# A two-layer scan kernel: planned times of layer 2's side steps moved by about one slot

## The chip, the cores and the metric

The kernel runs on one core of one Trainium2 chip. The metric is the device time of one launch in microseconds (us), over all 16 images. A core has TensorE (PE in the profile, its weight loads PEld), VectorE (DVE), ScalarE (ACT), GpSimd (POOL) and SyncE (SP), which here only issues DMAs. Each engine works through its own list of instructions in order and waits on semaphores.

## What is computed

The input is x of shape (16, 192, 56, 56). Layer 1 is group norm, an RWKV mixing layer and a residual add; the change does not touch it. Layer 2 is group norm and a Mamba block with a forward and a backward direction, and a residual add. Cut to what matters here:

```
tok = group_norm(x) as 3136 tokens of 192 channels
x1, x2 = layernorm(tok) * g + b                      # two pairs of g, b
x, z = x1 @ W_in_x.T, x2 @ W_in_z.T                  # 384 channels each
branch(x):                                           # once forward, once backward in time
    xc  = silu(conv_b + 4-tap convolution of x)
    dbl = xc @ W_xproj.T                             # 12 rows for dt, 16 for B, 16 for C
    dt  = softplus(dbl[:12] @ W_dt.T + dt_bias)
    h_t = h_(t-1) * exp(dt_t * A) + dt_t * xc_t * B_t  # 384 channels x 16 states
    y_t = sum over the states of h_t * C_t, + xc_t * D
out = x + ((y_forward + y_backward) * silu(z)) @ W_out.T + b_out
```

## The kernel before, in words

A loop over the 16 images holds two blocks, one for each layer; the engines meet between them. Layer 2 cuts the 3136 tokens into 7 chunks of T = 448 and goes over them forward (chunks i = 0 to 6) and then backward (i = 7 to 13): `CHUNK`, NI = 14. The 384 channels are EJ = 3 groups of 128 (e = 0, 1, 2). The 16 states of a group are NP = 8 **slots**, each of two states for 64 channels: an instruction has 128 partitions and 2 x 448 elements. So a chunk has PER = 24 slots, and an image Q = 336, numbered g. "Place n" below is the slot n of its chunk.

**The main line of a slot.** For pair q of slots:
- ScalarE, `decay` (L1294): two exponentials of dt * A, into one of two pairs of PSUM banks, one slot ahead of the scan; then `reset` (L1303) and `carry` (L1311), a few elements each. `decay(q)` waits for scan q-2.
- the product dt * xc * B: on VectorE for odd q (L1148, issued at slot q-2) and on GpSimd for even q (L1355, issued at slot q-3). It goes into one of NB = 4 buffers. VectorE's reads dt * xc from a PSUM bank, which a TensorE step `dp` (L985) fills once per group; GpSimd's reads it from SBUF, where a DMA `ud` (L1440) has spread it.
- VectorE, `scan` (L1159): the recurrence.
- GpSimd, `outputs` (L1364): h * C for two slots at once (q and q+1, q even), issued at slot q+2. It waits for both scans and, as its result has NPR = 4 slots of buffer, for TensorE's sum of the pair before the last (`c_sm >= q - 2`).
- TensorE, the **sum** (L1065), LAG = 2 slots behind: 8 matmul instructions add the two slots of a pair into the y bank, YBANK. A group begins there with the skip product xc * D (L1057), which waits until y of the group before has been read out, and ends, in backward chunks, with y of the forward direction added (L1060).

VectorE's slot is scan, then product (at odd slots), then side steps. ScalarE's is `decay(g+1)`, `reset`, `carry(g-1)`, side steps. GpSimd's is outputs (at even slots), product (at odd slots), side steps. TensorE's is the skip product and the sum (at odd slots), then side steps.

**The side steps** are all else. `side_schedule` gives each a planned time in slots by hand; each engine's list is sorted by it, and `Steps.due(g)` issues, at the end of slot g, what has a planned time below g + 1. So a shift of one slot changes what stands in front of what in an engine's list, and nothing is started by a clock. The steps of chunk i, with t the chunk's start, run while chunk i-1 is scanned:
- forward: `ns`, `n1`, `nc`, `nq`, `n2`, `nr`, `nm` (layer norm, on ScalarE, TensorE L992 and L998, VectorE L1096, ScalarE L1199, GpSimd L1338), `x` and `xe` (the projection L1004 and its copy), `nw`, `xw` (stores)
- both: `cv` (the convolution, 8 matmul instructions, L1018), `c1` to `c4` (ScalarE, L1220 to L1233), `xc` (VectorE, L1122), `xp` (TensorE, L1025), `p1` (ScalarE, L1240), `cw` (stores B and C), `bl` and `cl` (loads that spread them, L1418 and L1424), and for each group `t`, `t1` to `t3`, `td`, `du` (TensorE L1030, ScalarE L1247 to L1255, VectorE L1128, GpSimd L1344), `dd` and `de` (DMAs L1433 that spread dt), `ud` and `dp`
- backward: `z` with `z1` to `z4` and `g` (the gate: TensorE L1035, ScalarE L1266 to L1283, GpSimd L1348), `o` and `ou` (the output projection L1042 and its add, L1140), `xl`, `nl`, `yl`, `out` (loads and the store)
- `ye` reads y of a group out of YBANK: ScalarE (L1259) in forward chunks, VectorE (L1135) in backward ones. In both it waits for the last sum of its group.

Convolutions, projections and gates share two PSUM banks (6 and 7), which a loop at the end of `side_schedule` gives out in the order of the planned times; a step waits until the last reader of its bank is done.

Of the kernel before, what the change touches and what calls it, by code (L numbers as in the profile page):

```python
# [23 lines left out]
PER = EJ * NP  # L24
# [11 lines left out]


AHEAD, LAG = 2, 2
NB, NH, NPR = 4, 6, 4
NXC, NDT, NDU, NR2 = 5, 3, 3, 3  # L40

# [23 lines left out]
def side_schedule():  # L65


    pe, act, dve, pool, sp = [], [], [], [], []

    def conv(i, e, t):  # L70
        if (i, e) == (0, 0):
            dve.append((t, "cd", i, e))
        else:
            pe.append((t, "cv", i, e))
        act.extend([(t + 1.9, "c1", i, e), (t + 2.6, "c2", i, e), (t + 3.2, "c3", i, e), (t + 3.9, "c4", i, e)])
        dve.append((t + 4.6, "xc", i, e))

    def step_size(i, e, t):
        pe.append((t, "t", i, e))
        act.extend([(t + 1, "t1", i, e), (t + 2, "t2", i, e), (t + 2.6, "t3", i, e)])  # L80
        dve.append((t + 2.9, "td", i, e))
        pool.append((t + 3.9, "du", i, e))
        pe.append((max(NP * (EJ * i + e) - 2, t + 4.5), "dp", i, e))
        o = max(t + 3.4, NP * (EJ * i + e - 2) - 0.5 if i else t)
        sp.extend([(o, "dd", i, e), (o + 0.02, "de", i, e), (t + 4.4 if i or e else o + 0.01, "ud", i, e)])

    def project(i, t, u, v):

        pe.append((t, "xp", i, 0))
        act.append((t + v, "p1", i, 0))  # L90
        sp.append((t + 1.5, "cw", i, 0))
        for e in range(EJ):
            step_size(i, e, t + u[e] if i or not e else (-1.9, 1)[e - 1])
        for G in range(4):
            r = PER * i - NP + 2 * G if i else -100
            if i:
                sp.extend([(max(r + 1, t + 2), "bl", i, G), (max(r + 3, t + 2.1), "cl", i, G)])
            else:
                sp.extend([(t + (5.3 if G else 2) + G, "bl", i, G), (t + 5.9 + G, "cl", i, G)])

    def gate(i, e, t):
        pe.append((t, "z", i, e))
        act.extend([(t + 2, "z1", i, e), (t + 2.7, "z2", i, e), (t + 3.3, "z3", i, e), (t + 4, "z4", i, e)])
        pool.append((t + 4.8, "g", i, e))

    for i in range(NI):
        s = CHUNK[i][0]
        t = PER * (i - 1) - 2.5 * (i > 1) if i else -60
        if not s:
            act += [(t - 1.7, "ns", i, 0)]  # L110
            dve += [(t + 1.0, "nc", i, 0)]
            pe += [(t - 0.2, "n1", i, 0), (t + 2.1, "n2", i, 0)]
            act += [(t + 1.9, "nq", i, 0), (t + 3.0, "nr", i, 0), (t + 4.6, "xh", i, 0)]
            if i:
                pool += [(t + 3.4, "nm", i, 0)]
            else:
                dve += [(t + 1.9, "nq", i, 0), (t + 3.4, "nm", i, 0)]
            sp += [(t + 5, "nw", i, 0), (t + 8, "xw", i, 0)]
            for e, (u, v) in enumerate(((4.2, 6.4), (4.3, 8.6 if i > 1 else 7.4), (6.2, 11))):
                pe.append((t + u, "x", i, e))  # L120
                act.append((t + u + 1.2, "xe", i, e))
                conv(i, e, t + v)
            project(i, t + 15.6, (1.2, 1.7, 4.7), 1.2)
        else:
            sp += [(t - 8, "xl", i, 0), (t + 9, "nl", i, 0)]
            for e, v in enumerate((1.3, 6.0, 10.7)):
                conv(i, e, t + v)
            project(i, t + 15.6, (1.9, 2.3, 5.2), 1.5)
            t += 2.5
            gate(i, 0, t + 21.6)  # L130
            gate(i, 1, t + 26.4)
            gate(i, 2, t + 33.4)
            for k in range(CJ):
                o = t + 2 * PER + (6.4, 7.9)[k]
                pe.append((o, "o", i, k))
                dve.append((o + 1.5, "ou", i, k))
            sp.append((o + 2.5, "out", i, 0))
            sp.append((t + PER + 4, "yl", i, 0))
        for e in range(EJ):
            t = NP * (EJ * i + e + 1) + LAG - 1  # L140
            if not s:
                act.append((t + 0.9, "ye", i, e))
            else:
                dve.append((t + 1.5, "ye", i, e))
        if not s:
            sp.append((t + 1.5, "ys", i, 0))
    sp += [(PER * (NC - 2) + 13, "dg", 1, 0), (PER * (NI - 2) + 13, "dg", 0, 0)]
    dve += [(PER * (i + 2) + 12 if i < NI - 2 else Q + 5, "st", CHUNK[i][1], 0) for i in range(NC, NI - 1)]
    plans = [sorted(p, key=lambda a: a[0]) for p in (pe, act, dve, pool, sp)]
    jobs, used, until = {}, {}, {}  # L150
    last = dict(n1="nc", n2="nr", x="xe", cv="xc", xp="p1", t="td", z="z4", o="ou")
    read = {(name, i, e): t for p in plans[1:4] for t, name, i, e in p}
    release = {(name, i, e): read.get((last.get(name), i, e)) for _, name, i, e in plans[0]}
    for k, (t, name, i, e) in enumerate(a for a in plans[0] if a[1] != "dp"):
        banks = WBANK if t >= -10 else [*WBANK, 0, 1, 2, 3]
        b = banks[k % len(banks)] if t < -10 else min(banks, key=lambda n: until.get(n, -99))
        until[b] = release[name, i, e]
        jobs[name, i, e] = (k, b, used.get(b, 0))
        used[b] = used.get(b, 0) + 1
        if t < -10:  # L160
            first = dict(used)
    jobs["cv", 0, 0] = (None, DUBANK, 0)
    return plans, jobs, first
# [19 lines left out]
def build(nc, d, ctx):  # L183
# [708 lines left out]
    tmp = gz[0:CP, :, :]  # L892

    plans, jobs, first = side_schedule()
    plan_pe, plan_act, plan_dve, plan_pool, plan_sp = plans

# [650 lines left out]
```

## Time and profile before

| | us |
|---|---|
| median of 3 runs | 19903.05 |
| lowest, highest | 19885.40, 19917.42 |
| the profiled execution, its own time | 19868.46 |
| its span in the trace | 19866.7 |
| mean granted TensorE clock, share of full speed | 0.86 |
| VectorE busy, 13583 instructions | 17223.5 (87%) |
| GpSimd busy, 8340 instructions | 16549.9 (83%) |
| TensorE busy, 45152 matmul instructions | 15807.4 (80%) |
| ScalarE busy, 33157 instructions | 13148.7 (66%) |

How to read it: the span is that of one execution, from first to last instruction. A row of the timeline names an engine, a line of the kernel, what is written and read, and how many instructions are merged (x2); brackets give the idle time before it and what ended it, where "issue" means that no releaser is seen. Instructions of one engine overlap in the records by 0.04 to 0.10 us, so the distance between two starts is what an instruction costs its engine. A matmul of these 32-bit floats counts as two instructions.

### The profile page before, as it was taken

Reading aid. Unit: us, or ns where it says so; the run is one execution under the profiler, and the core shown is the slowest. Engines: PE = TensorE matmul, PEld = TensorE weight load, DVE = VectorE, ACT = ScalarE, POOL = GpSimd, SP = SyncE. Lnnn points to the kernel's source line nnn. Section 1 sums busy time; section 2 is a strip of 40 time slices with the busy share of each in tenths; the row PEclk is TensorE's granted clock in tenths of the full one; section 3 lists DMA queues with packets and bytes.
Section 4 is the critical chain, followed back from the end, with each engine's and each line's share of the span. In section 5 each row is a group of like instructions: output and inputs, shape, how many; then the busy total and the mean of one; then the engine's idle time right before and its main releaser. Section 6 shows DMA issues by size and latency. Waiting matters only on the chain. (4 is left out here: it accounts for less than half of the span.)

```text
span 19866.7 us, 185806 instructions
## 1 busy us (share of the span) xinstructions
PE 15807.4 (80%) x45152; PEld 5480.0 (28%) x45152; DVE 17223.5 (87%) x13583; ACT 13148.7 (66%) x33157; POOL 16549.9 (83%) x8340
## 2 busy tenths in 40 slices
PE   7887878878788787787878878888777877878878
PEld 2222222222222222222222222222222222222222
DVE  7988979889798897988979889798897988979889
ACT  5766657667676676766667666676666766667666
POOL 6978969789697896979969799697996978979789
PEclk8888888888888888888888888888888888888888
DMA  2424424244242442424424244242442424424244
GB/s 74 114 59 108 112 64 114 57 109 113 64 114 58 108 112 65 112 63 108 108 65 112 63 108 107 65 113 64 108 107 65 115 66 106 104 65 115 66 107 105
DMA packets 880267, 1820.05 MB, mean 92 GB/s; under 512 B 189530, under 2 KB 594804, under 8 KB 879028
## 3 DMA queue, kind: packets, MB, share of 16 engines
q1 hardware_dynamic: 879028, 1806.77, 36.0%
q8 instruction: 382, 6.26, 0.1%
q14 instruction: 857, 7.02, 0.1%
HBM read 1083.46 MB, written 245.63 MB: 67 GB/s over the span
## 5 line engine op out<-in xcount | busy, mean ns | idle before, releaser
L1159 DVE TENSOR_TENSOR_SCAN arena<-ps,arena 128x897 f32<-128x897 f32 x5376 | 10986.6, 2063 | 727.4 <-ACT arena L1311 637.1
L1364 POOL TENSOR_TENSOR arena<-arena 128x1792 f32<-128x1792 f32 x2688 | 9015.7, 3354 | 731.4 <-issue 573.2
L1294 ACT ACTIVATE ps<-arena,A 128x448 f32<-128x448 f32 x10752 | 6386.6, 627 | 2398.4 <-DVE arena L1159 2321.2
L1065 PE MATMUL ps<-arena,rep 128*64 128x448 f32 x21504 | 5668.9, 658 | 2358.9 <-POOL arena L1364 2351.3
L1355 POOL TENSOR_TENSOR arena<-arena 128x896 f32<-128x896 f32 x2688 | 4760.8, 1771 | 728.9 <-DMA arena<-arena 536.8
L1065 PEld LDWEIGHTS ps<-arena,rep 128*64 128x64 f32 x21504 | 1505.1, 156 | 6095.4 <-POOL arena L1364 3605.4
L1148 DVE TENSOR_TENSOR arena<-ps,arena 128x896 f32<-128x896 f32 x2688 | 2866.4, 1066 | 111.9 <-PE ps L985 99.1
L1018 PE MATMUL ps<-arena,diag 128*128 128x448 f32 x5248 | 2172.4, 557 | 57.1 <-DVE arena L1122 57.1
L1018 PEld LDWEIGHTS ps<-arena,diag 128*128 128x128 f32 x5248 | 977.6, 193 | 1236.3 <-issue 1051.8
L1057 PE MATMUL ps<-arena,skipd 128*128 128x448 f32 x1344 | 865.3, 733 | 525.8 <-DVE arena L1135 418.6
L1344 POOL TENSOR_TENSOR arena<-arena 128x448 f32<-128x448 f32 x672 | 654.6, 979 | 512.8 <-DVE arena L1128 512.8
L1311 ACT ACTIVATE arena<-arena 128x2 f32<-128x2 f32 x5376 | 1024.1, 191 | 53.3 <-DVE arena L1159 53.3
L1030 PE MATMUL ps<-arena,wdt 13*128 13x448 f32 x1344 | 763.7, 675 | 256.0 <-DVE arena L1128 244.4
L846 POOL TENSOR_TENSOR arena<-arena 128x448 f32<-128x448 f32 x336 | 344.5, 1025 | 731.6 <-DVE arena L592 731.6
L1303 ACT ACTIVATE arena<-arena 128x1 f32<-128x1 f32 x4608 | 869.0, 189 | 0.0
L985 PE MATMUL ps<-arena,rep 64*128 64x448 f32 x1344 | 714.1, 613 | 102.4 <-POOL arena L1344 57.1
L643 PE MATMUL ps<-x,arena 96*128 96x448 f32 x1344 | 675.6, 640 | 76.0 <-DVE arena L608 45.8
L1025 PE MATMUL ps<-arena,xpw 128*64 128x448 f32 x1344 | 711.0, 676 | 11.6 <-DVE arena L1122 11.6
L1122 DVE SCALAR_TENSOR_TENSOR arena<-ps,vece,arena 128x448 f32<-128x448 f32 x672 | 449.1, 668 | 300.4 <-ACT arena L1233 300.4
L621 DVE TENSOR_TENSOR_SCAN ps<-ps,arena 128x898 f32<-128x898 f32 x336 | 680.1, 2024 | 3.1
L1220 ACT ACTIVATE arena<-ps,vece 128x448 f32<-128x448 f32 x672 | 420.2, 625 | 376.3 <-PE ps L1018 374.3
L1004 PE MATMUL ps<-arena,wx 96*128 96x448 f32 x1344 | 614.2, 599 | 65.5 <-POOL arena L1338 55.6
(171 smaller groups left out, 19142.5 us busy)
## 6 DMA issues: line engine op xcount, KB each, us to landing
arena<-bc_rows SPq DMA_DIRECT2D x3584, 224.0 KB, 4.4
arena<-arena SPq DMA_DIRECT2D x4160, 112.0 KB, 2.3
x_projected<-arena SPq DMA_DIRECT2D x112, 672.0 KB, 3.6
y_forward<-arena SPq DMA_DIRECT2D x112, 672.0 KB, 4.6
arena<-x_projected SPq DMA_DIRECT2D x112, 672.0 KB, 4.8
arena<-y_forward SPq DMA_DIRECT2D x112, 672.0 KB, 5.4
x<-in_x SPq DMA_DIRECT2D x119, 336.0 KB, 3.6
x_normed<-arena SPq DMA_DIRECT2D x112, 336.0 KB, 4.0
```

The costliest lines, as they stand in the source:

```text
L985: e.matmul(ps[:, DUBANK, 0:T], rep[64:128, :], du[64:128, r % NDU, :], start=True, stop=True).then_inc(c_dp, 1)
L1018: m = e.matmul(o, diag[:, k, q, :], xh[i % 2][:, k, h:h + T], start=q == 0, stop=q == 3)
L1030: e.matmul(o, wdt[s][:, k * 128:(k + 1) * 128], res[0:R + 1, :], start=True, stop=True).then_inc(c_wt, 1)
L1057: e.matmul(y, skipd[:, s, k, :], xc[:, r % NXC, :], start=True, stop=False)
L1065: m = e.matmul(ps[64 * h:64 * h + 64, YBANK, 0:T], rep[:, 0:64], pr[:, (q - 1 + h) % NPR, a * T:a * T + T], start=False, stop=p == NP - 1 ...
L1148: e.tensor_tensor(two(bb[:, q % NB, :]), ps[:, DUBANK, 0:T].unsqueeze(1).to_broadcast([128, 2, T]), br[:, p - 1:p + 1, :], ALU.mult).then_ ...
L1159: e.tensor_tensor_scan(rev(hh[:, q % NH, 0:W2], s), rev(decays(q)[:, 0:W2], s), rev(bb[:, q % NB, 0:W2], s), car[:, 2 * k + p % 2, n:n + 1 ...
L1294: e.activation(two(decays(q))[:, a, :], dt2[:, r % NR2, p % 2, :], ACT.Exp, scale=Am[s][:, 2 * k + p % 2, n:n + 1]).then_inc(c_ex, 1)
L1303: e.activation(bb[:, q % NB, T:T1], car[:, 2 * k + p % 2, n:n + 1] if i % NC else zero[:, 0, 0:1], ACT.Copy).then_inc(c_rs, 1)
L1311: e.activation(car[:, 2 * k + p % 2, n:n + 2], h[:, 0:T1 + 1:T1] if s else h[:, T - 1:W2:T1], ACT.Copy).then_inc(c_ca, 1)
L1355: e.tensor_tensor(two(bb[:, q % NB, :]), du2[:, r % NR2, :].unsqueeze(1).to_broadcast([128, 2, T]), br[:, p:p + 2, :], ALU.mult).then_inc( ...
L1364: e.tensor_tensor(o.rearrange("p h (a b) -> p h a b", a=2), h.rearrange("p h (a b) -> p h a b", a=2)[:, :, :, 0:T], cr[:, p:p + 2, :].unsq ...
```

## The change

Times of chunks i > 1 start SOON = 3.5 slots early where they started 2.5 early, for backward chunks with the gates and outputs left where they were (`t += SOON`). Inside `project`, `t` steps, `p1` and what hangs on them are planned 0.5 slots later against the chunk's start in forward chunks (i > 1) and 0.2 later in backward ones (`p1`: 0.3), so they move by 0.5 to 0.8 slots against the main line. `ye` is planned 1.0 slot later on ScalarE and 0.7 later on VectorE, and the store `ys` 1.0 later. No instruction is added or removed, and no buffer.

```
--- before.py
+++ after.py
@@ -36,6 +36,7 @@
 
 
 AHEAD, LAG = 2, 2
+SOON = 3.5
 NB, NH, NPR = 4, 6, 4
 NXC, NDT, NDU, NR2 = 5, 3, 3, 3
 
@@ -105,7 +106,7 @@
 
     for i in range(NI):
         s = CHUNK[i][0]
-        t = PER * (i - 1) - 2.5 * (i > 1) if i else -60
+        t = PER * (i - 1) - SOON * (i > 1) if i else -60
         if not s:
             act += [(t - 1.7, "ns", i, 0)]
             dve += [(t + 1.0, "nc", i, 0)]
@@ -120,13 +121,13 @@
                 pe.append((t + u, "x", i, e))
                 act.append((t + u + 1.2, "xe", i, e))
                 conv(i, e, t + v)
-            project(i, t + 15.6, (1.2, 1.7, 4.7), 1.2)
+            project(i, t + 15.6, (1.7, 2.2, 5.2) if i > 1 else (1.2, 1.7, 4.7), 1.7 if i > 1 else 1.2)
         else:
             sp += [(t - 8, "xl", i, 0), (t + 9, "nl", i, 0)]
             for e, v in enumerate((1.3, 6.0, 10.7)):
                 conv(i, e, t + v)
-            project(i, t + 15.6, (1.9, 2.3, 5.2), 1.5)
-            t += 2.5
+            project(i, t + 15.6, (2.1, 2.6, 5.4), 1.8)
+            t += SOON
             gate(i, 0, t + 21.6)
             gate(i, 1, t + 26.4)
             gate(i, 2, t + 33.4)
@@ -139,11 +140,11 @@
         for e in range(EJ):
             t = NP * (EJ * i + e + 1) + LAG - 1
             if not s:
-                act.append((t + 0.9, "ye", i, e))
+                act.append((t + 1.9, "ye", i, e))
             else:
-                dve.append((t + 1.5, "ye", i, e))
+                dve.append((t + 2.2, "ye", i, e))
         if not s:
-            sp.append((t + 1.5, "ys", i, 0))
+            sp.append((t + 2.5, "ys", i, 0))
     sp += [(PER * (NC - 2) + 13, "dg", 1, 0), (PER * (NI - 2) + 13, "dg", 0, 0)]
     dve += [(PER * (i + 2) + 12 if i < NI - 2 else Q + 5, "st", CHUNK[i][1], 0) for i in range(NC, NI - 1)]
     plans = [sorted(p, key=lambda a: a[0]) for p in (pe, act, dve, pool, sp)]
```

## Rows read from the trace of the kernel before

**Rows 1.** The page's first part: busy time, share of the span, instructions
```profile
PE 15807.4 (80%) x45152; PEld 5480.0 (28%) x45152; DVE 17223.5 (87%) x13583; ACT 13148.7 (66%) x33157; POOL 16549.9 (83%) x8340
```

**Rows 2.** Stage windows of image 9, one per chunk: busy us (instructions), then clock, DMA
```profile
10480.10:10551.80 71.70, 56.85 (x165) 19.30 (x164) 64.72 (x45) 50.05 (x132) 65.44 (x30) 0.86 0.44 109
10551.80:10620.20 68.40, 53.55 (x152) 18.62 (x152) 63.47 (x44) 47.86 (x128) 63.96 (x29) 0.84 0.45 121
10620.20:10685.30 65.10, 52.65 (x154) 17.07 (x153) 63.16 (x44) 46.28 (x123) 60.03 (x26) 0.85 0.48 117
10685.30:10756.20 70.90, 56.02 (x160) 18.60 (x160) 62.77 (x46) 51.20 (x135) 67.21 (x31) 0.86 0.45 117
10756.20:10826.20 70.00, 58.36 (x175) 20.03 (x174) 66.00 (x49) 51.04 (x134) 65.87 (x31) 0.90 0.47 118
...
11041.70:11114.50 72.80, 58.05 (x169) 19.41 (x167) 67.16 (x50) 51.08 (x134) 66.50 (x31) 0.88 0.46 115
```

**Rows 3.** Timeline of ScalarE, forward chunk 4: start, us, line, [idle before <-releaser]
```profile
10509.06 0.54 ACT L1259 ACTIVATE arena<-ps 128x448 f32<-128x448 f32 x1 [3.71 <-PE ps L1065]
```

**Rows 4.** Timeline of TensorE in the same chunk
```profile
10504.06 3.27 PE L1018 MATMUL ps<-arena,diag 128*128 128x448 f32 x8 [0.29 <-DVE arena L1122]
10507.26 1.72 PE L1065 MATMUL ps<-arena,rep 128*64 128x448 f32 x8
...
10520.67 3.76 PE L1025 MATMUL ps<-arena,xpw 128*64 128x448 f32 x6
...
10544.77 2.96 PE L992 MATMUL ps<-arena,ones 96*96 96x448 f32 x4
```

**Rows 5.** Timeline of GpSimd in the same chunk
```profile
10514.22 3.36 POOL L1364 TENSOR_TENSOR arena<-arena 128x1792 f32<-128x1792 f32 x1 [2.70 <-issue]
...
10551.04 3.36 POOL L1364 TENSOR_TENSOR arena<-arena 128x1792 f32<-128x1792 f32 x1 [1.81 <-issue]
```

**Rows 6.** Timeline of VectorE in the same chunk
```profile
10511.40 0.68 DVE L1122 SCALAR_TENSOR_TENSOR arena<-ps,vece,arena 128x448 f32<-128x448 f32 x1 [2.43 <-ACT arena L1233]
```

**Rows 7.** Timeline of GpSimd, backward, chunk 9 into chunk 10
```profile
10894.95 1.77 POOL L1355 TENSOR_TENSOR arena<-arena 128x896 f32<-128x896 f32 x1 [2.74 <-DMA arena<-arena]
...
10918.72 3.36 POOL L1364 TENSOR_TENSOR arena<-arena 128x1792 f32<-128x1792 f32 x1
```

**Rows 8.** Timeline of SyncE's DMA issues in the same stretch
```profile
10889.83 2.52 SPq L1440 DMA_DIRECT2D arena<-arena  x4
```

**Rows 9.** Timeline of VectorE in the same stretch
```profile
10899.40 4.05 DVE L1159 TENSOR_TENSOR_SCAN arena<-ps,arena 128x897 f32<-128x897 f32 x2
10903.38 1.07 DVE L1148 TENSOR_TENSOR arena<-ps,arena 128x896 f32<-128x896 f32 x1
...
10909.34 0.62 DVE L1135 TENSOR_TENSOR arena<-arena,ps 128x448 f32<-128x448 f32 x1 [2.90 <-PE ps L1065]
```

**Rows 10.** Timeline of TensorE in the same stretch
```profile
10885.32 1.86 PE L1057 MATMUL ps<-arena,skipd 128*128 128x448 f32 x2 [3.29 <-DVE arena L1135]
...
10893.92 1.77 PE L1035 MATMUL ps<-arena,wz 96*128 96x448 f32 x4
10895.62 1.02 PE L985 MATMUL ps<-arena,rep 64*128 64x448 f32 x2
10896.57 3.27 PE L1018 MATMUL ps<-arena,diag 128*128 128x448 f32 x8
...
10910.01 1.02 PE L1057 MATMUL ps<-arena,skipd 128*128 128x448 f32 x2 [0.75 <-DVE arena L1135]
...
10912.47 1.72 PE L1065 MATMUL ps<-arena,rep 128*64 128x448 f32 x8
...
10920.77 2.50 PE L1042 MATMUL ps<-arena,wout 128*96 128x448 f32 x6 [0.78 <-ACT arena L1283]
```

**Rows 11.** Stage windows of that stretch; the first number behind POOL is the granted clock
```profile
10892.00:10905.60 13.60, 10.39 (x34) 3.67 (x32) 13.60 (x10) 11.51 (x32) 10.86 (x6) 1.00 0.73 170
10905.60:10909.00 3.40, 2.93 (x8) 0.77 (x8) 0.83 (x1) 2.17 (x6) 3.40 (x3) 0.51 1.03 237
```

More of the change, by code:

```diff
@@ L38 @@
 AHEAD, LAG = 2, 2
+SOON = 3.5
 NB, NH, NPR = 4, 6, 4
@@ L107, in side_schedule @@
         s = CHUNK[i][0]
-        t = PER * (i - 1) - 2.5 * (i > 1) if i else -60
+        t = PER * (i - 1) - SOON * (i > 1) if i else -60
         if not s:
@@ L122, in side_schedule @@
                 conv(i, e, t + v)
-            project(i, t + 15.6, (1.2, 1.7, 4.7), 1.2)
+            project(i, t + 15.6, (1.7, 2.2, 5.2) if i > 1 else (1.2, 1.7, 4.7), 1.7 if i > 1 else 1.2)
         else:
@@ L127, in side_schedule @@
                 conv(i, e, t + v)
-            project(i, t + 15.6, (1.9, 2.3, 5.2), 1.5)
-            t += 2.5
+            project(i, t + 15.6, (2.1, 2.6, 5.4), 1.8)
+            t += SOON
             gate(i, 0, t + 21.6)
@@ L141, in side_schedule @@
             if not s:
-                act.append((t + 0.9, "ye", i, e))
+                act.append((t + 1.9, "ye", i, e))
             else:
-                dve.append((t + 1.5, "ye", i, e))
+                dve.append((t + 2.2, "ye", i, e))
         if not s:
-            sp.append((t + 1.5, "ys", i, 0))
+            sp.append((t + 2.5, "ys", i, 0))
     sp += [(PER * (NC - 2) + 13, "dg", 1, 0), (PER * (NI - 2) + 13, "dg", 0, 0)]
```

## The prediction

> **What bounds the kernel now.** I read the busy shares first [rows 1]: VectorE 87% and GpSimd 83% of the span, both over two layers, so neither is the bound by that alone. Then I cut layer 2 of one image into its chunks [rows 2]. A chunk takes some 71 us, and GpSimd is busy for 65 to 67 us of it, VectorE for 63 to 67. The two are nearly equal, and 4 to 6 us of each chunk is idle time of both. The change can only win that. The timelines say where it sits, at the same places in each chunk of a kind.
>
> Forward chunks have two holes. At place 10 ScalarE's `ye` stands in its queue for 3.71 us and waits for TensorE's last sum of the group [rows 3]. That sum ran 7.26 to 8.98 (all at 10,500 us), as a convolution stood in front of it from 4.06 to 7.3 [rows 4]. Behind `ye` are the decays and the last steps of `xc`, so VectorE idles 2.43 us [rows 6] and then GpSimd 2.70 us [rows 5]. At place 22 VectorE's `nc` waits for the norm's matmul, which began only at 10,544.77, behind a sum [rows 4]; GpSimd loses 1.81 us by it [rows 5].
>
> Backward chunks have one main hole. At place 22 GpSimd's product waits 2.74 us for a DMA [rows 7], the `ud` issued from 10,889.83 on [rows 8]. Being late by it, GpSimd ends the outputs late, their sum is late, and VectorE's `ye` at place 2 waits 2.90 us [rows 9]. This is one loss seen twice.
>
> **The change, part by part.** Nothing is added or removed; all of it is order. I replayed one forward and one backward chunk, instruction by instruction, with the distances of the rows: scan 1.99 us (half of 4.05, less the overlap) and VectorE's product 0.98 [rows 9], GpSimd's outputs 3.31 [rows 5] and product 1.73 [rows 7], sum 1.65, convolution 3.2 [rows 4], gate matmuls `z` 1.7, `dp` 0.95, skip 0.9, output projection 2.4 [rows 10].
>
> *`ye` on ScalarE a slot later, forward.* It now stands behind the next decay, and the convolution, a slot sooner, ends before the sum is due. The sum then ends before ScalarE comes to `ye`. The 2.70 us go. The next skip product waits for `ye`, but the sum behind it must wait for GpSimd anyway, so that costs nothing.
>
> *Norm chain a slot sooner.* `n1` moves in front of a sum, into time in which TensorE waits for GpSimd, so `nc` no longer waits. `nm` is then next: it needs `n2` and `nr`, and GpSimd waits for it 0 to 1.7 us. `xp`, 3.76 us at half clock [rows 4], comes a slot sooner than the sum and ScalarE's `p1` may hold a decay for about 0.6 us. Together a chunk of 71.7 us becomes 67.1 to 68.4, a gain of 3.3 to 4.6. I take 4.2 for chunks 2 to 4. Chunks 1 and 5 have only one of the two holes in full: 3.0 each; chunk 0 0.5. Sum 19.1 us per image. `ns` and the stores `nw`, `xw`, `cw`, `ys` move on queues with room.
>
> *`ud` sooner.* In backward chunks SyncE now issues it in front of one `bl` and one `cl`, four DMA issues of some 0.6 us (four took 2.52 [rows 8]): 2.5 us sooner, which nearly closes the 2.74. `bl` and `cl` behind it are wanted later. In chunks 6 and 7 this is a gain. I take 2.0 each of the 2.7, so 4.0.
>
> *Convolutions sooner, backward.* Here the order of TensorE gets worse, since gates and `dp` stay where they are. I count from the start of slot 234 (10,882.14), in chunks 8 to 12.
> - Slot 237/238: the order was z, dp, cv [rows 10]; it becomes z, cv, dp, as 237.8 is now below dp's 238. `dp` ended at 14.4, and VectorE's product that reads it began at 16.3, 0.98 before the scans of [rows 9]. So there are 1.9 us of slack for 3.2 us of convolution. With VectorE's own phase in the replay the wait is 2.4 us.
> - Slot 242/243: z and sum and then cv [rows 10] become z, cv, sum. GpSimd's outputs of slot 246, at 10,918.72 [rows 7], need that sum, which ended at 10,914.1: 4.6 us of slack. But `ye` (below) releases skip, z, cv and sum in a row.
> - Slot 247: cv comes before the second `o`, and VectorE's `ou` waits 1.4 us. The first `ou` waits 0.8.
>
> *`ye` on VectorE a slot later.* It goes behind another scan and a product, 2.97 us, and its wait of 2.90 goes. The skip product of the next group waits for it. In the replay `ye` ends at 30.0. Skip, z, cv and sum take 7.3 us at full clock, so the sum ends at 37.3. VectorE's scan that the outputs also need ends at 34.0. GpSimd waits 3.3 us.
>
> *The clock's share.* TensorE has nothing from 22.9 to 30.0 in the replay. In the trace 3.31 and 3.29 us without work were followed by half clock (1.2 of 2.4 GHz): granted 0.51 over 10,905.6 to 10,909.0 [rows 11], and a skip of 1.86 us instead of 1.02 [rows 10]. With skip and z at half clock the sum ends at 39.9, and GpSimd waits 5.9 us. The second `dp` stands behind this sum, and VectorE waits for it 0.8 (full clock) to 3.5 us (half).
>
> The Trainium skill (TensorE: Matmul & The Clock Gate, Part 1: The HAM clock gate) says that the array's default state is throttled and that activity releases it. That rule speaks against this change, which lengthens a stretch without activity; by it alone a backward chunk would be at the half-clock end below, and the total near 19,810.
>
> *A backward chunk.* VectorE's work is 59.5 us (24 scans, 12 products) and 7.3 us for 11 side steps and two statistics, 66.8. Waits: 2.4 + 3.5 + 0.8 + 1.4 = 8.1 at half clock, so 75 us; 2.4 + 0.8 + 0.8 + 1.4 = 5.4 at full clock, so 72.3. Chunks 8 to 12 take 71.7 on average now (10,756.2 to 11,114.5 [rows 2]). I take 74.4, nearer to half clock as both idle stretches of the rows ended in it. That is +2.7 for each of five chunks, +13.5. Chunk 13 has no convolution behind it: 0.
>
> *Sum.* -19.1 - 4.0 + 13.5 = -9.6 us per image, times 16 images -154. The profiled execution took 19,868, so 19,714; the median of the runs is 35 above it, so 19,750.
>
> **The rivals.** (1) *Full clock, and the gains whole.* The clock stays up or rises soon after `ye`; backward chunks take 72.5 (+0.8 x 5), forward chunks gain 4.6 x 3 + 6.5, chunks 6 and 7 together 5. -21.3 x 16 = -341: 19,562. For: between 10,892.0 and 10,905.6 the clock was full at the same load [rows 11]. Against: the longer idle stretch.
>
> (2) *TensorE's queue decides in backward chunks: slower.* One mechanism, the late sum at slot 242/243. If skip, z and the whole convolution (6.3 us instead of 3.2) run at half clock, the sum ends at about 42, and `dp`, both `o` and both `ou` follow 2 to 3 us later again. A chunk then takes 78 us, +6.3 x 5 = +31; with forward gains of only 16 and 2 for chunks 6 and 7 this is +13 x 16 = +208: 20,111. It decides from +4.6 us per backward chunk on (23.1 / 5). For: rows 10 show a chain of work without a gap there already. Against: GpSimd's 2.7 us won just before give some of it back.
>
> (3) *Nothing in sum.* The forward holes close but `nm`, `xp` and `dp` open others of the same size, or the two halves cancel: 19,903. Gains of 12 and losses of 12 would do it.
>
> **Chances.** The forecast 0.38, (1) 0.27, (2) 0.22, (3) 0.13. The forecast's own range is 19,620 to 19,850. Eight in ten: from 19,490, some 70 below (1), to 19,990, which takes in (3) and the mild end of (2). About 0.2% (40 us) is what a measurement of this kernel can tell from no change. Faster 0.65, within 0.13, slower 0.22.
>
> **What would show it.** Right: no ScalarE row of L1259 at place 10 with a wait of over 1 us; GpSimd's idle 2.7 at place 11 and 1.8 at place 23 of forward chunks gone, those chunks at 67 to 69 us; GpSimd's DMA wait at place 22 of backward chunks below 0.5 us. VectorE's product L1148 waiting for L985 at place 23, GpSimd's L1364 waiting for a sum at place 6, 3 to 6 us, and backward chunks at 73 to 76 us. Wrong: backward chunks at or below 71 us (then the sum was not late, look at when `ye` ends), or forward chunks at 70 or above (then look at `nm` and `p1`).

## The result, and the profile after

| | us |
|---|---|
| before, median of 19 runs | 19893.09 |
| after, median of 19 runs | 19925.64 |
| ratio, 95% interval | 1.0015, 1.0008 to 1.0022 |

The change makes the kernel 0.15% slower. The prediction was 19,750, faster by 0.7%. The profiled execution after has a span of 19,908.6 us against 19,866.7. Behind this small difference stand large ones of opposite sign, which the chunks show. The stage windows of the same image, for chunks 3 to 12 after the change (columns as in [rows 2]):

```profile
10417.70:10484.70 67.00, 53.36 (x164) 18.43 (x164) 64.16 (x45) 50.72 (x132) 65.38 (x30) 0.92 0.43 112
10484.70:10551.00 66.30, 55.10 (x164) 18.57 (x164) 64.22 (x45) 50.56 (x132) 65.38 (x30) 0.90 0.43 115
10551.00:10618.90 67.90, 53.96 (x162) 19.16 (x164) 63.31 (x44) 49.21 (x131) 66.30 (x30) 0.90 0.51 136
10618.90:10686.70 67.80, 48.21 (x150) 16.18 (x148) 62.85 (x43) 46.64 (x124) 65.95 (x28) 0.90 0.48 119
10686.70:10756.30 69.60, 53.80 (x162) 19.36 (x160) 62.89 (x46) 51.63 (x136) 65.50 (x30) 0.85 0.44 113
10756.30:10834.80 78.50, 61.15 (x176) 21.87 (x174) 66.14 (x49) 51.27 (x134) 66.77 (x31) 0.83 0.42 106
10834.80:10913.30 78.50, 61.22 (x176) 21.84 (x174) 67.20 (x51) 51.34 (x134) 65.70 (x31) 0.83 0.41 104
10913.30:10991.80 78.50, 61.29 (x176) 21.86 (x174) 67.20 (x51) 51.35 (x134) 66.52 (x31) 0.85 0.43 104
10991.80:11067.60 75.80, 57.31 (x176) 20.82 (x174) 67.00 (x50) 51.26 (x134) 65.59 (x31) 0.89 0.44 108
11067.60:11142.70 75.10, 57.28 (x166) 19.91 (x164) 67.08 (x50) 49.62 (x129) 64.46 (x30) 0.84 0.41 104
```

Forward chunk 4, 71.7 us in [rows 2], takes 66.3, and GpSimd is busy for 65.4 of it: the holes are nearly shut. Backward chunks 8 to 12, 71.7 on average, take 75 to 78.5. Averaged over all 16 images, from the first scan of a chunk to the first of the next:

```
chunk       0     1     2     3     4     5     6     7     8     9    10    11    12    13
before   78.7  78.1  72.9  72.2  71.7  68.3  65.1  70.8  70.5  72.8  71.4  71.7  72.2  67.1
after    81.4  73.7  66.6  66.7  66.9  67.6  66.2  70.2  75.7  78.4  78.5  75.8  75.1  65.6
```

Chunks 1 to 5 win 21.8 us, chunk 0 loses 2.7, chunks 6 and 7 together lose 0.5, chunks 8 to 12 lose 24.8, chunk 13 wins 1.5. What lies between layer 2's scans of two images is 2.2 us shorter. In sum +2.5 us per image, 40 in all.

That last stretch is mostly layer 1, whose work and plan are the same in every kernel here, so its 2.2 us are no direct gain of the moves. Over the 195 such stretches of the thirteen traces its length goes with TensorE's granted clock between 20 and 40 us into it (correlation -0.93). After the change all fifteen take 234 us, with 0.62 there. Before it ten take 235 with 0.58 to 0.61, and three take 239 to 241 with 0.50. The window of one image after the change, and of one of experiment 3, where the stretches take 239 to 242:

```profile
11227.80:11247.80 20.00, 16.75 (x55) 9.42 (x56) 8.67 (x18) 5.45 (x13) 3.97 (x5) 0.62 0.01 2
11266.30:11286.30 20.00, 16.65 (x49) 8.59 (x50) 7.49 (x16) 3.19 (x9) 3.74 (x4) 0.50 0.01 2
```

So a total can shift by up to some 6 us per image, 0.5%, through a layer that the change does not touch. Layer 2 by itself is 4.7 us per image longer. What sets the clock in that window is not shown.

**Where the time in backward chunks goes.** VectorE's timeline from place 23 of chunk 9 to place 9 of chunk 10, as in [rows 9]:

```profile
10912.28 1.09 DVE L1149 TENSOR_TENSOR arena<-ps,arena 128x896 f32<-128x896 f32 x1 [2.78 <-PE ps L986]
...
10923.78 0.61 DVE L1136 TENSOR_TENSOR arena<-arena,ps 128x448 f32<-128x448 f32 x1
...
10934.17 2.08 DVE L1160 TENSOR_TENSOR_SCAN arena<-ps,arena 128x897 f32<-128x897 f32 x1 [4.83 <-ACT arena L1312]
10937.47 2.08 DVE L1160 TENSOR_TENSOR_SCAN arena<-ps,arena 128x897 f32<-128x897 f32 x1 [1.21 <-ACT arena L1312]
...
10941.58 0.68 DVE L1141 SCALAR_TENSOR_TENSOR x<-ps,bout,x 96x448 f32<-96x448 f32 x1 [0.45 <-PE ps L1043]
...
10949.15 0.68 DVE L1141 SCALAR_TENSOR_TENSOR x<-ps,bout,x 96x448 f32<-96x448 f32 x1 [1.94 <-PE ps L1043]
```

The product waits 2.78 us for `dp`, which now stands behind a convolution. `ye` (L1136) waits for nothing. Then the scan of place 6 waits 4.83 and that of place 7 1.21 us, for ScalarE. The two `ou` (L1141) wait 0.45 and 1.94. TensorE in that stretch, as in [rows 10]:

```profile
10906.52 1.77 PE L1036 MATMUL ps<-arena,wz 96*128 96x448 f32 x4
10908.13 3.17 PE L1019 MATMUL ps<-arena,diag 128*128 128x448 f32 x8
10911.23 1.02 PE L986 MATMUL ps<-arena,rep 64*128 64x448 f32 x2
...
10924.45 1.86 PE L1058 MATMUL ps<-arena,skipd 128*128 128x448 f32 x2 [7.80 <-DVE arena L1136]
10926.10 3.00 PE L1036 MATMUL ps<-arena,wz 96*128 96x448 f32 x4
10928.94 3.17 PE L1019 MATMUL ps<-arena,diag 128*128 128x448 f32 x8
10932.04 3.23 PE L1066 MATMUL ps<-arena,rep 128*64 128x448 f32 x16
```

It has nothing for 7.80 us and then skip, gate matmul and convolution in a row, 7.6 us, before the sum. The granted clock was 0.51 during skip and gate matmul and 1.00 from the convolution on:

```profile
10924.45:10928.90 4.45, 4.45 (x6) 2.18 (x7) 4.45 (x3) 0.00 (x0) 4.08 (x2) 0.51 0.00 0
10928.90:10935.20 6.30, 6.30 (x26) 2.39 (x24) 1.47 (x2) 4.15 (x10) 1.23 (x1) 1.00 0.01 3
```

GpSimd, and ScalarE, behind them:

```profile
10933.97 3.36 POOL L1365 TENSOR_TENSOR arena<-arena 128x1792 f32<-128x1792 f32 x1 [5.44 <-PE ps L1066]
```

```profile
10929.14 0.64 ACT L1267 ACTIVATE arena<-ps,bxz 128x448 f32<-128x448 f32 x1 [4.81 <-PE ps L1036]
10929.67 0.60 ACT L1268 ACTIVATE ps<-ps,bxz 128x448 f32<-128x448 f32 x1
10932.15 0.64 ACT L1221 ACTIVATE arena<-ps,vece 128x448 f32<-128x448 f32 x1 [1.87 <-PE ps L1019]
10932.68 1.19 ACT L1295 ACTIVATE ps<-arena,A 128x448 f32<-128x448 f32 x2
```

GpSimd's outputs wait 5.44 us for that sum. ScalarE waits 4.81 us for the gate matmul in `z1` and 1.87 for the convolution in `c1`, and only then comes the decay that VectorE's scan wants.

### The profile page after: what moved, and what is told of

Its sections match the earlier page's. It is cut to its first block and busy times, and to the rows that moved or that the text cites. A ratio compares the mean times of both kernels' runs of the same rounds, so it can differ in the third digit from the quotient of the medians.

```text
span 19908.6 us, 185806 instructions
## 1 busy us (share of the span) xinstructions
PE 15550.0 (78%) x45152; PEld 5506.3 (28%) x45152; DVE 17179.5 (86%) x13583; ACT 13222.8 (66%) x33157; POOL 16607.8 (83%) x8340
## 5 line engine op out<-in xcount | busy, mean ns | idle before, releaser
L1066 PEld LDWEIGHTS ps<-arena,rep 128*64 128x64 f32 x21504 | 1578.5, 156 | 4609.6 <-issue 2904.1
L1058 PE MATMUL ps<-arena,skipd 128*128 128x448 f32 x1344 | 1001.6, 839 | 2140.6 <-DVE arena L1136 1486.6
L1058 PEld LDWEIGHTS ps<-arena,skipd 128*128 128x128 f32 x1344 | 267.9, 249 | 2692.9 <-DVE arena L1136 1744.9
L1221 ACT ACTIVATE arena<-ps,vece 128x448 f32<-128x448 f32 x672 | 423.9, 631 | 660.8 <-PE ps L1019 657.7
L1005 PE MATMUL ps<-arena,wx 96*128 96x448 f32 x1344 | 656.5, 635 | 173.5 <-POOL arena L1339 164.1
L1031 PE MATMUL ps<-arena,wdt 13*128 13x448 f32 x1344 | 707.0, 620 | 100.9 <-DVE arena L1129 89.4
L1036 PE MATMUL ps<-arena,wz 96*128 96x448 f32 x1344 | 736.7, 681 | 0.0
L1043 PE MATMUL ps<-arena,wout 128*96 128x448 f32 x1344 | 612.7, 599 | 127.0 <-ACT arena L1284 127.0
```

The lines of the kernel that those rows point to most:

```text
L1031: e.matmul(o, wdt[s][:, k * 128:(k + 1) * 128], res[0:R + 1, :], start=True, stop=True).then_inc(c_wt, 1)
L1036: m = e.matmul(o, wz[:, j, k * 128:(k + 1) * 128], nrm[:, i % 2, j * T:j * T + T], start=j == 0, stop=j == 1)
L1058: e.matmul(y, skipd[:, s, k, :], xc[:, r % NXC, :], start=True, stop=False)
L1066: m = e.matmul(ps[64 * h:64 * h + 64, YBANK, 0:T], rep[:, 0:64], pr[:, (q - 1 + h) % NPR, a * T:a * T + T], start=False, stop=p == NP - 1 ...
```

## The experiments

Each was timed against the kernel before in runs on the same chip; medians of before in those jobs lay between 19,916 and 19,930, so ratios are the better measure. "Chunks 8 to 12" is their mean over all images (before 71.7, after 76.7).

**1. Undo the convolutions' move in backward chunks.**

```
-            for e, v in enumerate((1.3, 6.0, 10.7)):   # backward
+            for e, v in enumerate((2.3, 7.0, 11.7)):
```

> The changed kernel, but with the convolutions of backward chunks planned one slot later again (2.3, 7.0, 11.7 in place of 1.3, 6.0, 10.7), so that on TensorE dp stands in front of the convolution at place 22 and the sum in front of it at place 3. Theory A (the order on TensorE makes backward chunks slow): GpSimd's idle 5.4 us at place 5 and VectorE's 2.8 at place 23 go, chunks 8 to 12 fall from 76.7 us on average to 70 to 72, the total to about 19,470. Rival B (the late read of y on VectorE is the cause by itself, the convolution only adds its 3.2 us): chunks 8 to 12 at 73 to 74.5, the total at about 19,670.

Measured 19,539, ratio 0.9811 (0.9795 to 0.9827). Chunks 8 to 12: 72.4. That is close to theory A, just above its 70 to 72, and below B's 73 to 74.5. Something of the loss is left: in chunk 10 ScalarE's `c1` (L1221) still waits for the convolution, as the late `ye` holds up the TensorE steps that stand in front of it, and the decay behind `c1` keeps VectorE waiting. ScalarE and VectorE of this run:

```profile
10717.46 0.63 ACT L1221 ACTIVATE arena<-ps,vece 128x448 f32<-128x448 f32 x1 [2.34 <-PE ps L1019]
```

```profile
10719.95 2.08 DVE L1160 TENSOR_TENSOR_SCAN arena<-ps,arena 128x897 f32<-128x897 f32 x1 [3.08 <-ACT arena L1312]
```

**2. Undo VectorE's `ye` move.**

```
-                dve.append((t + 2.2, "ye", i, e))
+                dve.append((t + 1.5, "ye", i, e))
```

> The changed kernel, but VectorE's ye planned where it was before (1.5 in place of 2.2). Theory A: the convolution still stands in front of the sum, but skip, gate matmul, convolution and sum start some 3 us sooner and TensorE idles less in front of them; GpSimd's 5.4 us at place 5 fall to between 0 and 2.5, chunks 8 to 12 come to 72 to 74, the total to 19,550 to 19,700. Rival B: nothing is left of the loss but the wait for dp, chunks 8 to 12 at 70 to 71.5, the total at about 19,450. Rival C (the place of ye is of no account, since it waits for its sum anyhow): 76 to 77 and 19,925.

Measured 19,700, ratio 0.9891 (0.9875 to 0.9908). Chunks 8 to 12: 74.4; GpSimd's wait at place 5 is 3.0 to 3.2 us. Rival C is out, B too. A is nearest, at the upper edge of its total, with the wait above its 2.5 us and the chunks above its 74: undone alone, this gives back less than the convolutions' move.

**3. `dp` in front of the convolution.**

```
-        pe.append((max(NP * (EJ * i + e) - 2, t + 4.5), "dp", i, e))
+        pe.append((max(NP * (EJ * i + e) - (2.25 if i >= NC and not e else 2), t + 4.5), "dp", i, e))
```

> The changed kernel, but the first dp of a backward chunk is planned in front of the convolution (order z, dp, cv). VectorE's wait of 2.8 us for L986 at place 23 must go. If it is on the path: 2.7 us in each of chunks 6 to 11, 16 images, 260 us, so 19,665. If the late sum at place 5 sets the pace and what VectorE wins is waited away there: 0 to 60 us, 19,870 to 19,925.

Measured 20,004, ratio 1.0037 (1.0026 to 1.0049): slower than the change itself. The wait for `dp` is gone, and VectorE's timeline shows where its 2.78 us went:

```profile
10949.50 1.09 DVE L1149 TENSOR_TENSOR arena<-ps,arena 128x896 f32<-128x896 f32 x1
10950.51 2.07 DVE L1160 TENSOR_TENSOR_SCAN arena<-ps,arena 128x897 f32<-128x897 f32 x1
10954.73 2.08 DVE L1160 TENSOR_TENSOR_SCAN arena<-ps,arena 128x897 f32<-128x897 f32 x1 [2.15 <-ACT arena L1312]
...
10974.21 2.08 DVE L1160 TENSOR_TENSOR_SCAN arena<-ps,arena 128x897 f32<-128x897 f32 x1 [5.39 <-ACT arena L1312]
```

2.15 us at place 1, where ScalarE's `c1` waits for the convolution in front of a decay, and 0.56 more at place 6. So the wait for `dp` was real but cost nothing that the next wait would not have taken: chunks 9 and 10 take 78.5 us, as in the changed kernel. The expectation's second branch holds in kind; that the run is 78 us slower, and not 0 to 60 faster, it did not foresee. By the two traces most of this is not in layer 2: its scans take only 1.4 us per image longer (22 us in all; chunk 8 is 2.6 longer, chunk 6 as much shorter), while the stretch of layer 1 takes 239.4 in place of 234.1, with the low clock shown above, some 80 us over the fifteen such stretches.

**4. The forward part alone.**

```
+SOON_B = 2.5
-        t = PER * (i - 1) - SOON * (i > 1) if i else -60
+        t = PER * (i - 1) - (SOON if i < NC else SOON_B) * (i > 1) if i else -60
...
-            project(i, t + 15.6, (2.1, 2.6, 5.4), 1.8)
-            t += SOON
+            project(i, t + 15.6, (1.9, 2.3, 5.2), 1.5)
+            t += SOON_B
...
-                dve.append((t + 2.2, "ye", i, e))
+                dve.append((t + 1.5, "ye", i, e))
```

> The change in forward chunks alone: backward chunks start 2.5 slots early, with the projection's times and VectorE's ye as before. Chunks 1 to 5 keep what they gained (21.8 us per image), chunk 0 its loss (2.7), chunks 7 to 13 are as before: 19,893 less 16 x 19 = 19,590. If instead the forward part's gain hangs on the backward part, or is paid back at the turn (chunks 5 to 7): above 19,750.

Measured 19,545, ratio 0.9812 (0.9795 to 0.9828), 45 us below the expected 19,590. Chunks 1 to 5: 73.6, 66.7, 66.6, 66.9, 66.0; chunks 8 to 12: 71.8, as before. Each half acts on its own chunks: the forward part wins 1.9%, and the backward part loses 2.0%.

**5. The forward part, and of the backward part the DMA alone.**

```
-            (t + 4.4 if i or e else o + 0.01, "ud", i, e)
+            (t + (3.9 if i >= NC and not e else 4.4) if i or e else o + 0.01, "ud", i, e)
```

> The forward part of the change alone, and in backward chunks only one more thing: the first ud of a chunk is planned half a slot sooner, so that SyncE issues it in front of one bl and one cl. Theory (GpSimd's wait of 2.7 us for that DMA at place 22 is on the path in backward chunks): chunks 6 to 12 lose 1.5 to 2.7 us each against the forward part alone (19,545), the total at 19,240 to 19,380. Rival (VectorE's 66.8 us of work and the order of TensorE's queue bound these chunks, so the wait only moves): 0 to 0.5 us a chunk, 19,490 to 19,545.

Measured 19,141, ratio 0.9603 (0.9587 to 0.9619): **4.0% faster than before**, 100 us more than expected at best. It is the fastest kernel of this study, with experiment 11. Chunks 6 to 12: 64.3, 66.1, 68.0, 68.5, 68.5, 68.2, 68.2. Stage windows of chunks 9 and 10, then SyncE and GpSimd at the place of [rows 7, 8]:

```profile
10432.40:10500.30 67.90, 56.76 (x174) 19.55 (x174) 66.84 (x51) 51.05 (x134) 65.53 (x31) 0.92 0.48 121
10500.30:10568.50 68.20, 59.49 (x176) 20.31 (x175) 66.80 (x50) 51.03 (x134) 66.48 (x31) 0.87 0.49 121
```

```profile
10483.47 5.03 SPq L1435 DMA_DIRECT2D arena<-arena  x8
10488.55 1.25 SPq L1442 DMA_DIRECT2D arena<-arena  x2
10489.84 1.24 SPq L1426 DMA_DIRECT2D arena<-bc_rows  x2
```

```profile
10490.08 3.35 POOL L1366 TENSOR_TENSOR arena<-arena 128x1792 f32<-128x1792 f32 x1
10493.39 1.77 POOL L1357 TENSOR_TENSOR arena<-arena 128x896 f32<-128x896 f32 x1
```

`ud` (L1442) is issued right behind the spreads of dt, in front of `bl` and `cl`, and the product (L1357) follows GpSimd's outputs with no gap where 2.74 us stood [rows 7]. VectorE is busy for 66.8 of 68.2 us: these chunks now stand at its work. The gain is larger than GpSimd's wait, which was 2.6 us on average in chunk 10. With it went other waits of VectorE, above all that of `ye` at place 2 (2.90 us), and its idle time in chunk 10 fell from 4.4 to 1.6 us.

**6. ScalarE's `z1` and `c1` behind the decay of place 6** (in the changed kernel).

```
-    act.extend([(t + 1.9, "c1", i, e), ...
+    act.extend([(t + (2.55 if i > NC and e == 1 else 1.9), "c1", i, e), ...
-        act.extend([(t + 2, "z1", i, e), ...
+        act.extend([(t + (2.6 if e == 1 else 2), "z1", i, e), ...
```

> The changed kernel, but on ScalarE z1 and c1 of the second group stand behind the decay of place 6 and no longer in front of it. They wait for the late gate matmul and convolution, and the decay behind them with them: VectorE's 4.8 us at place 6. Theory (this queue is the term that the prediction left out): the decay of place 6 is free, the stall moves to place 7 and shrinks to what dp costs, chunks 8 to 12 lose 2 to 3 us each, the total at 19,690 to 19,770. Rival (GpSimd's wait for the sum sets the pace by itself, at 5.4 us): under 0.5 us a chunk, 19,890 to 19,926.

Measured 19,757, ratio 0.9909 (0.9893 to 0.9926), in the range of the theory. Chunks 8 to 12: 74.7, 2.0 less. As expected the wait moved by one scan and became one of 4.70 where there were 4.83 and 1.21. GpSimd's wait for the sum is the same, 5.31 us, yet the chunk is shorter: so that wait does not set the pace by itself. What is left of VectorE's wait is still ScalarE's: `z1` and `c1` now stand in front of the decay of place 7.

```profile
10853.63 2.08 DVE L1160 TENSOR_TENSOR_SCAN arena<-ps,arena 128x897 f32<-128x897 f32 x1 [4.70 <-ACT arena L1312]
```

```profile
10851.44 3.36 POOL L1365 TENSOR_TENSOR arena<-arena 128x1792 f32<-128x1792 f32 x1 [5.31 <-PE ps L1066]
```

**7. TensorE kept at work in the idle stretch** (in the changed kernel; the nine matmuls write into a bank that the gate matmul then overwrites).

```
                 if p == 0:
+                    if NC <= i < NI - 1 and k == 0:
+                        job("z", i, 1)
+                        busy(e, 9, bank_of("z", i, 1))
                     y_free(w, r)
```

> The changed kernel, and TensorE runs nine matmuls of no use into the gate's bank in the 7.8 us in which it waits for ye in chunks 7 to 12 (the result is not changed by them). If the half clock behind that idle stretch costs what the trace shows (skip and z at 7.60 us with the convolution where 5.6 are due), the sum at place 3 ends 2.0 us sooner and chunks 8 to 12 lose 1.5 to 2 us each: 19,765 to 19,805. Rival (the order alone, the clock does not count): 19,910 to 19,930. If the nine run past the end of ye, slower than 19,926.

Measured 19,890, ratio 0.9984 (0.9974 to 0.9994). TensorE of this run:

```profile
10877.08 6.07 PE L631 MATMUL ps<-skipd,ident 128*128 128x384 f32 x18 [1.07 <-ACT arena L1287]
10883.77 1.02 PE L1061 MATMUL ps<-arena,skipd 128*128 128x448 f32 x2 [0.61 <-DVE arena L1139]
10884.62 1.67 PE L1036 MATMUL ps<-arena,wz 96*128 96x448 f32 x4
10886.13 3.17 PE L1019 MATMUL ps<-arena,diag 128*128 128x448 f32 x8
10889.23 3.23 PE L1069 MATMUL ps<-arena,rep 128*64 128x448 f32 x16
```

The clock share is as large as expected at its place: skip 1.02 in place of 1.86 us, the gate 1.67 in place of 3.00, from skip to sum 5.5 in place of 7.6, GpSimd's wait 3.31 in place of 5.44. The granted clock is 1.00 where it was 0.51:

```profile
10883.77:10886.10 2.33, 2.33 (x6) 1.24 (x7) 2.33 (x2) 0.00 (x0) 2.33 (x2) 1.00 0.00 0
```

VectorE's wait at place 6 of chunk 10 falls by the whole 2.1 us, from 4.80 to 2.69 on average, but waits at other places grow (the scan of place 15 waits 1.0, the first `ou` 0.9 in place of 0.5), and chunks 8 to 12 get shorter by 1.3 us each (75.4). Chunk 7 gets longer by 2.1. There TensorE's stretch without work was only 4.5 us, and the nine matmuls outlast it: skip starts 12.4 us behind the chunk's first scan in place of 6.6, and VectorE's wait at place 6 grows from 0.9 to 3.0. All in all the run is 0.3% faster. Neither branch of the expectation fits: the clock counts, for some 100 us in chunks 8 to 12 and 60 in the total, not 120 to 160.

**8. ScalarE's `ye` where it was** (in the forward part alone).

```
-                act.append((t + 1.9, "ye", i, e))
+                act.append((t + 0.9, "ye", i, e))
```

> The forward part alone, with ScalarE's ye planned where it was (0.9 in place of 1.9). Theory (the read of y in front of a decay is what cost 2.7 us at place 10): chunks 1 to 5 grow by 2 to 2.7 us each, 12 us per image, the total at 19,545 + 190 = 19,735. Rival (the convolution a slot sooner has already freed TensorE for the sum, so ye waits for little wherever it stands): under 0.7 us a chunk, below 19,600.

Measured 19,596, ratio 0.9831 (0.9815 to 0.9848), 0.2% above experiment 4. The rival is right: `ye` waits 0.63 us at its old place, where it waited 3.71 [rows 3]. The convolution still stands in front of the sum, but in chunk 4 of the same image it starts 0.1 us behind the scan of place 8, where it started 2.7 behind it, and the sum is sooner by as much.

```profile
10350.87 0.54 ACT L1261 ACTIVATE arena<-ps 128x448 f32<-128x448 f32 x1 [0.63 <-PE ps L1067]
```

Chunks 2 to 4 take 67.7 us in place of 66.7 (before 72.3). Of the gain of 5.5 us a chunk, 1.0 is `ye`'s and 4.5 that of the norm chain, convolutions and projection moved together; no run separates these.

**9. The DMA alone** (the kernel before, with the line of experiment 5).

> The kernel before, with the one move of ud alone (first ud of a backward chunk half a slot sooner). Theory: what it won on top of the forward part (404 us, chunks 7 to 13 from 71.0 to 67.3 us) it wins here too, since backward chunks are the same: 19,480 to 19,540. Rival: it needs the forward part, whose last chunks hand over to the backward ones with less delay: above 19,650.

Measured 19,554, ratio 0.9809 (0.9794 to 0.9824): half a slot less in the planned time of one DMA wins 1.9%, 14 us short of the expected range. Chunk 6 stays at 65.1, chunk 7 falls from 70.8 to 66.8, chunks 8 to 12 to 68.4. Layer 2 by itself is 24.2 us per image shorter, 387 us in all; in this trace the stretch of layer 1 is 4.3 us longer. The forward part (20.9 us per image of layer 2 in experiment 4) and this DMA add up to nearly what both together win (47.2 in experiment 5). GpSimd's waits for that kind of DMA over the whole run, by the page's groups of experiment 5 and of this one:

```profile
L1357 POOL TENSOR_TENSOR arena<-arena 128x896 f32<-128x896 f32 x2688 | 4759.7, 1771 | 408.2 <-DMA arena<-arena 229.8 <-DMA arena<-bc_rows 107.6 <-DVE arena L1161 64.6
```

```profile
L1355 POOL TENSOR_TENSOR arena<-arena 128x896 f32<-128x896 f32 x2688 | 4761.4, 1771 | 382.5 <-DMA arena<-arena 202.6 <-DMA arena<-bc_rows 107.7 <-DVE arena L1159 66.5
```

Before, the same group waited 536.8 us for it: 334 us less of waiting, some 375 less of time. Of the 203 us that stay, 151 are in chunk 0 of the images and 50 in front of their first scans.

**10. Both backward moves undone** (experiments 1 and 2 together).

> The changed kernel, with both backward moves undone: convolutions one slot later again and VectorE's ye where it was. What stays of the backward part is ud, dd, t, p1 and cw sooner. Theory (the two moves together are the whole loss, and hide the gain by ud): chunks 8 to 12 at 67.5 to 69.5 us, the total at 19,100 to 19,220. Rival (another of the backward moves costs too): chunks 8 to 12 above 70.5, the total above 19,350.

Measured 19,217, ratio 0.9634 (0.9619 to 0.9649), in the expected range. Chunks 8 to 12: 68.9. With experiment 4 this splits the backward part: the rest of it (`ud` and the projection sooner) wins 1.8%, and the two moves together cost 3.8%. With either one undone the other still costs: the convolutions' 2.6% by themselves (experiment 2 against 10), `ye` 1.8% by itself (1 against 10).

**11. Chunk 2 as before** (experiment 5 with `SOON if 2 < i < NC`, and the projection's times with `i > 2`).

> The forward part with ud (19,141), and chunk 2 started 2.5 slots early as before. Theory (chunk 2's chain, a slot sooner, runs into the ends of chunk 1's in chunk 0, which grew from 78.7 to 81 us): chunk 0 falls to 79 and chunk 1 stays at 73.6, total 19,100 to 19,120. Rival (chunk 0 and chunk 1 only trade): chunk 1 grows by what chunk 0 loses or more, 19,141 to 19,200.

Measured 19,144, ratio 0.9606 (0.9593 to 0.9619): no difference from experiment 5. Chunk 0 falls from 80.6 to 79.6, chunk 1 stays at 73.7. That is the theory in kind, but the 16 us that it would bring are below what can be told here, and chunk 0 lies between 80.1 and 82.0 in the other traces with the forward part, so it stays open.

## Why the prediction was wrong, point by point

- **Forward chunks: right in sum, partly by luck.** 19.1 us per image were forecast, and 21.8 less the 2.7 of chunk 0 came. Chunks 2 to 4 won 16.6 where 12.6 were taken, and went to 66.7, below the 67.1 to 68.4 of the replay. Chunk 1 won 4.4 for 3.0, but chunk 5 only 0.7 for 3.0, and chunk 0 lost 2.7 where it was to win 0.5. The prediction closed the hole of place 10 by two moves, `ye` a slot later and the convolution a slot sooner. By experiment 8 the steps a slot sooner do most of it, and `ye`'s own move is worth 1.0 us a chunk.
- **`ud` sooner: right in its place.** GpSimd's DMA wait at place 22 is gone, and by itself the move wins the forecast 4.0 us in chunks 6 and 7, all of it in chunk 7 (experiment 9). But in the changed kernel these two chunks lost 0.5 us: the prediction priced the wait for `dp` in chunks 8 to 12 alone, and here too VectorE waits for it at place 23, 3.3 and 3.2 us. How much of this gain the rest hid the prediction did not see: by itself this DMA is worth 1.9% of the kernel.
- **The order at slot 237/238: right in size, 2.4 forecast and 2.78 measured**, and yet no cause by itself: taken away, it came back in the next wait (experiment 3).
- **The late sum: right.** 5.9 us were forecast for GpSimd at half clock and 5.44 measured; `ye` waits for nothing; the two `ou` wait 0.45 and 1.94 (forecast 0.8 and 1.4).
- **The step that failed: what VectorE waits for behind the late sum.** The prediction had 3.5 us, for the second `dp`, and let ScalarE's decays come on time. The product that reads the second `dp` waits for nothing in the trace. ScalarE's queue has `z1` and `c1` in front of the decay of place 6. They read what TensorE does behind the skip, so the decay comes late, and VectorE waits 4.83 + 1.21 us. Experiment 6 moved those two steps behind that decay, with GpSimd's wait as it was, and got 2.0 us a chunk back. With 2.78 + 4.83 + 1.21 and the two `ou` (0.45 and 1.9) the waits are 11.2 us, and with 66.8 of work this is 78, as measured in chunks 9 and 10. The prediction had 8.1 and 75, and then took 74.4, leaning to full clock. Measured were 76.7 on average. Of the 12.1 us per image between forecast (-9.6) and result (+2.5), chunks 8 to 12 are 11.3 and chunks 6 and 7 are 4.5; 3.7 came back in chunk 13 and in layer 1, where the prediction had nothing.
- **The clock: right in kind.** After 7.80 us without work skip and gate ran at half clock (granted 0.51), as the prediction had it. The Trainium skill's rule (TensorE: Matmul & The Clock Gate, Part 1: The HAM clock gate), that the default state is throttled and activity releases it, agrees with experiment 7: with matmuls of no use in that stretch skip took 1.02 us in place of 1.86. The clock's share of the total is 0.3% by experiment 7, and experiments 1 and 2 show that order weighs more.
- **Rival 2 came nearest, and not by its own route.** It named the late sum behind TensorE's queue and the point from which that decides, 4.6 us per backward chunk; 5.0 were measured. But it made up its price of 6.3 from a convolution at half clock, which ran at full clock (3.17 us), and from `dp`, `o` and `ou` coming later; of ScalarE it says nothing. Its forward gain, 16 + 2, was near the truth (21.8 - 2.7 - 0.5).
- **Small slips in its sums.** A chunk of 75 us gives a total near 19,800, not 19,810, and with the convolution at half clock rival 2's sum would end at 43, not 42 (39.9 + 3.1). Neither changes the outcome.

Not settled: what sets the clock at the start of layer 1, and why chunk 0 grows by 2.7 us. For chunk 0 the trace names the place: at place 19 VectorE's `td` (L1129) waits 3.1 us on average for ScalarE's `t3`, where before it hardly waited; in experiment 11 it waits 1.3.

## What to carry to other kernels

When a read of a result is put later to spare its own engine a wait, list what the reader releases, and what stands in each queue behind that: here VectorE's `ye` released a TensorE chain, and two ScalarE steps reading that chain stood in front of the work that VectorE needed next. When a plan holds several moves, split it by stage before judging it: a total of +0.15% hid -1.9% and +2.0%, and the half that lost hid a gain of 1.8%. A DMA that one engine waits for at the same place of every chunk is worth a look at the order of the issuing queue first; half a slot in one planned time gave 1.9%. And when a difference is a few tenths of a per cent, look first at whether it lies in the part that was changed.

## What the runs showed of the hardware that was not expected

The granted clock of a stretch whose work is the same came out differently from kernel to kernel: 0.50 to 0.62 between 20 and 40 us into layer 1, and the stretch took 234 to 246 us with it. In the changed kernel it was 0.62 in all fifteen stretches and in experiment 3 0.50 in all; before the change and in most experiments it changed from image to image.

That the waits behind a half-clock stretch can be shortened by matmuls of no use was expected; that 2.1 us shorter at one place of a chunk came out as 1.3 in its length shows how much of such a gain other queues hold back.
